# Window attention on one core: where the group statistic stands on VectorE, and which engine adds the bias of V

## The reference

```
x = x + _L0_conv_ref(_gn(x), L0_conv_w_qkv, L0_conv_b_qkv)

def _gn(v, G=32, eps=1e-05):
    g = v.reshape(B_, G, C_ // G, H_, W_)
    m = jnp.mean(g, axis=(2, 3, 4), keepdims=True)
    s = jnp.var(g, axis=(2, 3, 4), keepdims=True)
    return ((g - m) / jnp.sqrt(s + eps)).reshape(v.shape)

# _L0_conv_ref: roll by -3, -3; then
    qkv = jnp.einsum('bchw,oc->bohw', xs, w_qkv) + b_qkv[None, :, None, None]
    # cut into windows of 49 tokens and 8 heads
    scores = jnp.einsum('bxyhqd,bxyhkd->bxyhqk', q, k) * scale
    attn = jax.nn.softmax(scores, axis=-1)
    out = jnp.einsum('bxyhqk,bxyhkd->bxyhqd', attn, v)
    # back to b, c, h, w; roll by 3, 3
```

## Time and profile before

| | |
|---|---|
| median of 3 runs | 941.21 us (940.23 to 943.64) |
| the profiled execution | 941.08 us |
| its span, first to last instruction | 938.9 us |
| granted TensorE clock, mean | 0.99 |
| TensorE busy | 865.0 us, 92% |
| VectorE busy | 766.3 us, 82% |
| GpSimd busy | 739.3 us, 79% |
| ScalarE busy | 665.1 us, 71% |

### The profile page before, as it was taken

One profiled execution on the slowest core, in us unless ns is written; L12 is line 12 of the kernel. 1 busy time (PEld: TensorE's weight loads), 2 busy tenths in 40 slices (PEclk: granted clock), 3 DMA queues, 4 the chain that ended last, 5 costly groups with the idle time before them and its releaser, 6 DMA issues. The chain is left out here.

```text
span 938.9 us, 104445 instructions
## 1 busy us (share of the span) xinstructions
PE 865.0 (92%) x46473; PEld 708.7 (75%) x46473; DVE 766.3 (82%) x1399; ACT 665.1 (71%) x1297; POOL 739.3 (79%) x1191
## 2 busy tenths in 40 slices
PE   0479999998999999999999999999899999999994
PEld 0358888887788888887788888887678888888883
DVE  8657888889889888888888888888987777777873
ACT  2347777776677777777677777777677777777772
POOL 1347888887788888888788888888788888888883
PEclk9999999999999999999999999999999999999998
DMA  9401122112112211221211000000000000000001
GB/s 380 177 5 58 46 68 68 60 42 69 48 55 68 69 43 60 68 68 34 69 54 50 35 34 34 17 34 34 17 34 35 19 32 34 34 22 29 34 34 36
DMA packets 29912, 51.87 MB, mean 55 GB/s; under 512 B 3649, under 2 KB 28865, under 8 KB 29761
## 3 DMA queue, kind: packets, MB, share of 16 engines
q1 hardware_dynamic: 29888, 51.59, 15.8%
HBM read 25.89 MB, written 25.69 MB: 55 GB/s over the span
## 5 line engine op out<-in xcount | busy, mean ns | idle before, releaser
L373 ACT ACTIVATE probs_t<-psum,exp_scale 128x800 f32<-128x800 f32 x256 | 223.2, 923 | 139.6 <-PE psum L772 139.6
L571 DVE TENSOR_REDUCE neg_max<-psum 100x16 f32<-100x784 f32 x256 | 249.2, 974 | 39.1 <-PE psum L740 31.1
L291 POOL TENSOR_SCALAR mixed<-mixed,bias 128x392 f32<-128x392 f32 x128 | 161.7, 1263 | 123.2 <-DVE mixed L597 123.2
L740 PEld LDWEIGHTS psum<-k_hi,q_masks 32*128 32x128 f16 x8192 | 175.3, 91 | 46.3 <-issue 42.8
L740 PE MATMUL psum<-k_hi,q_masks 32*128 32x49 f16 x8192 | 197.8, 179 | 3.0 <-DVE neg_max L571 2.3
L740 PE MATMUL psum<-k_lo,q_masks 32*128 32x49 f16 x4096 | 182.6, 179 | 0.0
L740 PEld LDWEIGHTS psum<-k_lo,q_masks 32*128 32x128 f16 x4096 | 161.0, 91 | 0.0
L300 POOL TENSOR_TENSOR stage<-mixed,image 128x343 f32 (+7 forms) x256 | 144.2, 583 | 0.4 <-POOL mixed L291 0.4
L765 PE MATMUL psum<-q_masks,k_hi 32*64 32x100 f16 x8192 | 128.7, 219 | 16.1 <-DVE summed L588 13.3
L349 ACT ACTIVATE xn<-image,shift_c,rstd_c 128x21 f32 (+6 forms) x256 | 132.4, 573 | 8.0 <-DVE shift_c L551 6.1
L797 PE MATMUL psum<-probs_t,v_rows 64*32 64x100 f32 x8192 | 131.4, 252 | 2.4 <-issue 2.4
(11 more groups left out here) (112 smaller groups left out, 1828.2 us busy)
## 6 DMA issues: line engine op xcount, KB each, us to landing
out_dram<-stage SPq DMA_DIRECT2D x64, 224.0 KB, 2.1
out_dram<-stage SPq DMA_DIRECT2D x64, 168.0 KB, 1.9
image<-in_x_dram SPq DMA_DIRECT2D x32, 224.0 KB, 2.6
image<-in_x_dram SPq DMA_DIRECT2D x1, 6104.0 KB, 28.2
image<-in_x_dram SPq DMA_DIRECT2D x34, 168.0 KB, 2.5
image<-in_x_dram SPq DMA_DIRECT2D x6, 896.0 KB, 9.2
image<-in_x_dram SPq DMA_DIRECT2D x1, 728.0 KB, 14.3
w_nat<-in_L_conv_w_qkv_dram SPq DMA_DIRECT2D x1, 192.0 KB, 2.4
```

Source lines behind the costliest of these rows:

```text
L291: nc.gpsimd.tensor_scalar(mixed[:, half, :, :], mixed[:, half, :, :], bias[:, 2:3], None, ALU.add).then_inc(bias_added, 1)
L373: nc.scalar.activation(probs_t[:, 2 * u:2 * u + 2, :, :].rearrange("p h a q -> p h (a q)"), psum[:, COL_BANKS[u], 0:PAIRS * ROWS2], ACT.Ex ...
L571: nc.vector.tensor_reduce(neg_max[:, par, 2 * j:2 * j + 2, :], psum[0:ROWS2, ROW_BANKS, 0:GT] .rearrange("p h (w k) -> p h w k", k=TOK), A ...
L740: last = nc.tensor.matmul(psum[:, ROW_BANKS.start + h - 2 * j, w * TOK:(w + 1) * TOK], q_masks[rows, par, low + w * ROWS2:low + w * ROWS2 ...
```

## The change

Three things change.

1. On VectorE the statistic, and the pieces of the image change, stand behind `scale_rows`, directly ahead of the second maximum. Before, the statistic and one kind of piece stood behind the mask of Q, and another kind between `low_inverse` and `join`.
2. The image change begins two steps earlier and has one piece in each step, where six steps had up to two each. Its arithmetic is the same. Of the chunks of images 2 and 3, four steps now take two, where it was two steps.
3. The bias of V is added by ScalarE, in step g for group g-3, between the turned maximum and the exponentials. GpSimd adds the image to group g-4 in place of g-3, so each engine's program has one step more at the end.

```
@@ gpsimd
-            def add_bias(g, half):
-                pool.wait_ge(mixed_done, g + 2)
-                pool.sem_inc(waited, 1)
-                nc.gpsimd.tensor_scalar(mixed[:, half, :, :], mixed[:, half, :, :], bias[:, 2:3], None, ALU.add).then_inc(bias_added, 1)
...
             def step(g, n, par):
-                if live(g - 3):
-                    add_bias(g - 3, 1 - par)
                 if live(g - 1):
                     split_max(g - 1, 1 - par)
                 if live(g):
                     split_k(g, par)
-                if live(g - 3):
-                    add_image(g - 3, n - 2 + par, 1 - par)
+                if live(g - 4):
+                    add_image(g - 4, n - 2, par)
@@ scalar
+            def add_bias(g, half):
+                act.wait_ge(mixed_done, g + 2)
+                nc.scalar.activation(mixed[:, half, :, :], mixed[:, half, :, :], ACT.Identity, bias=bias[:, 2:3]).then_inc(bias_added, 1)
...
                     evac_neg(g - 1)
+                if live(g - 3):
+                    add_bias(g - 3, 1 - par)
                 if live(g - 1):
                     exp(g - 1, 0)
                     exp(g - 1, 1)
@@ vector
+            def norm_steps(b):
+                return [lambda: gather_channels(b), turn_channels, group_mean, group_variance] + NEWTON * [refine_root] + [lambda: offer(b)]
...
                 if live(g):
                     mask_q(g, par)
-                if ahead:
-                    ahead()
-                for chunk in chunks:
-                    take_stats(image_at + chunk * STAT, chunk)
                 if live(g - 2):
                     invert(g - 2)
                     low_inverse(g - 2)
-                if between:
-                    between()
...
                 if live(g - 2):
                     scale_rows(g - 2, par)
+                if ahead:
+                    ahead()
+                for chunk in chunks:
+                    take_stats(image_at + chunk * STAT, chunk)
                 if live(g):
                     maximum(g, par, 1)
...
             def change_image(b):
-                g = (b * BANDS - 4) * 2
-                for ahead, between in ((None, lambda: gather_channels(b)),
-                                       (turn_channels, group_mean),
-                                       (group_variance, guess_root),
-                                       (lambda: refine_root(1), lambda: refine_root(1)),
-                                       (lambda: refine_root(NEWTON - 2), scatter_groups),
-                                       (None, lambda: offer(b))):
-                    step(g, g // 2, g & 1, ahead=ahead, between=between)
-                    g += 1
+                first = (b * BANDS - 5) * 2
+                for g, piece in enumerate(norm_steps(b), first):
+                    step(g, g // 2, g & 1, ahead=piece)
...
-                for n in range(3):
+                for n in range(4):
                     dve.wait_ge(loaded[b + 1], 32 * -(-(2 * n + 2) * STAT // BAND))
                     two_steps(first + n, 2 * n, at)
                 dve.wait_ge(loaded[b + 1], 32 * BANDS)
-                for g in (2 * first + 6, 2 * first + 7):
-                    chunk = 6 + 2 * (g & 1)
-                    step(g, g // 2, g & 1, (chunk, chunk + 1), at)
-                with dve.Fori(4, CHUNKS // 2 - 1) as n:
-                    two_steps(n + first, 2 * n + 2, at)
+                with dve.Fori(4, CHUNKS // 2 - 4) as n:
+                    two_steps(n + first, 2 * n, at)
+                for n in (CHUNKS // 2 - 4, CHUNKS // 2 - 3):
+                    for par in range(2):
+                        chunk = CHUNKS - 8 + 4 * (n - CHUNKS // 2 + 4) + 2 * par
+                        step(2 * (first + n) + par, first + n, par, (chunk, chunk + 1), at)
```

More of the change, by code:

```diff
@@ L311, in step @@
                     split_k(g, par)
-                if live(g - 3):
-                    add_image(g - 3, n - 2 + par, 1 - par)
+                if live(g - 4):
+                    add_image(g - 4, n - 2, par)
                 if live(g + 2):
                     split_x(g + 2, par)
-            for g in range(-2, 4):
+            for g in range(-2, 6):
                 step(g, g // 2, g & 1)
-            with pool.Fori(2, GROUPS // 2 - 1) as n:
+            with pool.Fori(3, GROUPS // 2 - 1) as n:
                 step(2 * n, n, 0)
@@ L323, in _ @@
             pool.sem_inc(x_split, 1)
-            for g in range(GROUPS - 2, GROUPS + 3):
+            for g in range(GROUPS - 2, GROUPS + 4):
                 step(g, g // 2, g & 1)
@@ L423, in _ @@
                     step(2 * n + 1, n, 1, b)
-            for g in range(GROUPS - 2, GROUPS + 2):
+            for g in range(GROUPS - 2, GROUPS + 3):
                 step(g, g // 2, g & 1)
@@ L521, in group_mean, with refine_root, offer @@
                 link(nc.vector.tensor_tensor(work_b[:, :], work_a[:, :], work_a[:, :], ALU.mult))
+                link(nc.vector.tensor_tensor(work_a[:, :], work_b[:, :], var_row[:, :], ALU.add))
             def group_variance():
-                link(nc.vector.tensor_tensor(work_a[:, :], work_b[:, :], var_row[:, :], ALU.add))
                 link(nc.vector.tensor_reduce(g_var[:, :], grouped(work_a), AX.X, ALU.add))
                 link(nc.vector.tensor_scalar(g_var[:, :], g_var[:, :], 1.0 / PER, EPS, ALU.mult, ALU.add))
-            def guess_root():
                 link(nc.vector.tensor_scalar(half_bits[:, :], g_var[:, :].bitcast(i32), 1, None, ALU.logical_shift_right))
                 link(nc.vector.tensor_scalar(rs[:, :].bitcast(i32), half_bits[:, :], -1.0, float(0x5F3759DF), ALU.mult, ALU.add))
[L534 to L541, removed]
+            def refine_root():
+                link(nc.vector.tensor_tensor(rs_t[:, :], rs[:, :], rs[:, :], ALU.mult))
+                link(nc.vector.scalar_tensor_tensor(rs_t[:, :], rs_t[:, :], -0.5, g_var[:, :], ALU.mult, ALU.mult))
+                link(nc.vector.scalar_tensor_tensor(rs[:, :], rs_t[:, :], 1.5, rs[:, :], ALU.add, ALU.mult))
+            def offer(b):
+                wait(dve, xn_ready, (b - 1) * 2 * BANDS)
                 nc.vector.tensor_scalar(grouped(mean_row), g_sum[:, :, None].broadcast_to([C, 8, PER]), 1.0 / PER, None, ALU.mult)
                 link(nc.vector.tensor_scalar(grouped(var_row), rs[:, :, None].broadcast_to([C, 8, PER]), X_SCALE, None, ALU.mult))
-            def offer(b):
-                wait(dve, xn_ready, (b - 1) * 2 * BANDS)
                 nc.vector.transpose(mean_c[:, :], mean_row[:, :])
@@ L599, in scale_rows, with step @@
                                         summed[:, :, :].rearrange("p (s a) q -> p s a q", s=2), ALU.mult).then_inc(mixed_done, 1)
-            def step(g, n, par, chunks=(), image_at=None, ahead=None, between=None):
+            def step(g, n, par, chunks=(), image_at=None, ahead=None):
                 if live(g):
                     mask_q(g, par)
-                if ahead:
-                    ahead()
-                for chunk in chunks:
-                    take_stats(image_at + chunk * STAT, chunk)
                 if live(g - 2):
@@ L650, in _ @@
                     take_stats(chunk * STAT, chunk)
[L651 to L658, removed]
+            for piece in norm_steps(0):
+                piece()
             work_out_scales()
@@ L663, in _ @@
             step(1, 0, 1, range(5, 8), BANDS * BAND)
[L664 to L667, removed]
+            step(2, 1, 0, (8,), BANDS * BAND)
+            step(3, 1, 1, (9,), BANDS * BAND)
+            with dve.Fori(2, BANDS - 5) as n:
+                two_steps(n, 2 * n + 6, BANDS * BAND)
             for b in (1, 2):
```

## The result

The changed kernel takes 950.56 us, median of 4 runs (949.47 to 951.74), against 940.86 for the kernel before: a ratio of 1.0091, 95% interval 1.0064 to 1.0118. It is slower by 0.9%; forecast was 950.0. The profiled execution has a span of 948.9 us, 10.0 more than before.

The account below looks back on a forecast made before the run. TensorE's own order was taken to set a 6.69 us floor, exceeded by a 6.34 us loop plus pieces. 941.1 + 11.2 + 5.9 + 9.0 + 0.4 - 16.75 - 0.8 gave 950.0 us, range 935 to 959.

Parts of the forecast that it names:

- The loop: Row scores through second maximum and K's split to row scores: 6.34 us plus the inserted piece, against a 6.69 floor.
- The sum: Profiled execution 941.1 us plus 8.9: single statistics +11.2, doubles +5.9, image changes +9.0, start +0.4, removed waits -16.75, end -0.8.
- c: Time from the second maximum's end to the end of `k_lo` on GpSimd: 2.56 us, bounds 2.37 and 2.60.
- What goes: The 16.75 us lost in steady running disappear, as `join` no longer stands behind pieces.
- The bias on ScalarE: One more ScalarE operation, about 0.6 us, before the exponentials where it idles 0.95: no cost; later stores and loads not felt.
- The ends: First steps +0.4 us, bounds 0 and 2, mostly covered by code loads; end -0.8 from the shorter bias operation.
- What the profile would show: Periods 6.88, 7.4 and 6.9 to 7.3; some 25 us of TensorE waits naming `k_lo`; chain through L571, L282, L275.
- (A): Rival: GpSimd's split of the maximum gets in between the masks, 2.37 us to `k_lo`'s end; faster, 932.6 us; chance 0.15.
- (B): Rival: `inv_rows` on VectorE delays GpSimd's `k_lo` by 0.3 us in 17 steps; +5, 955 us; chance 0.11.

Follow-up runs that it names:

- e5: The changed kernel with each statistic taken over 224 columns in place of 448; 933.25 us, 0.9908 of the kernel before.
- e3: The changed kernel with GpSimd's split of K ahead of its split of the maximum; 927.62 us, 0.9819 of the kernel before.
- e1: The changed kernel with the bias of V back on GpSimd, one group earlier; 945.07 us, 1.0020 of the kernel before.
- e10: The kernel before with the bias on ScalarE, image added one group later, VectorE's full load wait and double statistics two steps later; 936.35 us, ratio 0.9936.
- e2: The kernel before with only the bias moved to ScalarE and the image added one group later; 944.67 us, ratio 1.0020.
- e4: The changed kernel with the statistics back behind the mask of Q; 934.10 us, 0.9889 of the kernel before.
- e13: The changed kernel plus one useless bias-sized GpSimd operation (1.26 us) in every step; 946.15 us, 1.0047 of the kernel before.

## Why the prediction was right

The forecast was 950.0, measured 950.56. By its own steps:

- **The loop, 6.34 us plus the piece.** Right in each term to 0.02. The rows above give 0.81 to the first maximum, 1.43 to `mixed`, 0.47 to the statistic; `k_lo` ends 2.57 after the maximum (forecast 2.56), the row scores follow 0.10 after it. e5 puts the threshold between 0.30 and 0.53, and the line through the points that cost at 0.35; e3 confirms that the way goes through GpSimd's order. A statistic counts 0.53 here, where 0.545 was taken from the start.
- **The sum.** Steps with one statistic 58 x 0.18 = 10.4 for 11.2; steps with two 8 x 0.71 = 5.6 for 5.9; three changes 9.3 for 9.0; 25.3 in all for 26.1, less 16.75. The single pieces came out nearly as priced: gathering takes 0.94 (period 7.29), turning 0.58, group mean and variance 0.89 and 0.83, the refinements 0.59 each (period 6.94 to 6.95) and the offer 0.71.
- **c, the disputed term.** Its value was right, and that it grows when the bias leaves. It was under-explored on the other side: with the bias on GpSimd and the statistic in its new place it is 2.26 (e1), less than my lower bound of 2.37.
- **What goes.** Right: `summed` is down to 0.8 us of waits, once.
- **The bias on ScalarE.** It takes 0.62 to 0.63 and costs ScalarE nothing: the idle time before the exponentials fell from 0.95 to 0.43, and e10 holds 6.69. That SP's and the loads' shift is not felt is right for this change only because the full wait moved along; e2 shows its price otherwise, two steps 3.8 and 4.2 us too long.
- **The ends.** The end is right, -0.8, and for the reason given: the image addition starts 0.83 after `mixed` ends, where it took 1.66. The sum behind step 127 by itself would not show it: e4 and e5 end in the same steps and have 24.9 and 23.3 us there. The start is mis-sized: +2.3 for +0.4, just over my bound of 2; that loads of code cover most of the moved statistics is shown by no run here. In step 1 TensorE waits 3.8 us for the low half of K in one piece; how much of the 2.3 that makes is open (see below). The errors of the start and of the sum (1.9 and -0.8) partly cancel; that the time came out closer than its terms is luck.
- **What the profile would show.** Periods as written. The names were wrong: I expected 25 us of waits put down to `k_lo`, and the view shows 3.8, once. The chain that ended last was to pass through L571, L282 and L275; the page of the profile puts 90% of it on TensorE and 0% on GpSimd. And `neg_halves` takes 0.56 in about half of the steps only. In the others it starts 0.34 instead of 0.18 after the maximum and takes 0.41; it ends 0.75 after the maximum in both.
- **Rivals.** (A) is refuted by c = 2.57 in the changed kernel; its mechanism is real and appears in e1 and e13. (B) does not happen as priced. In a step with two statistics `inv_rows` is asked for while GpSimd works on K's high part, ahead of `k_lo`:

```profile
402.19 0.28 DVE L576 SCALAR_TENSOR_TENSOR inv_rows<-inv_hi,low_rows,inv 128x49 f16<-128x49 f16 x1 [0.30 <-ACT inv_hi L381]
```

```profile
401.88 0.53 POOL L273 TENSOR_SCALAR k_hi<-k 128x392 f16<-128x392 f32 x1
402.50 0.90 POOL L275 TENSOR_TENSOR k_lo<-k,k_hi 128x392 f16<-128x392 f32 x1
```

It takes 0.28 and begins 0.31 into `k_hi`; neither delays the other, and it has just ended when `k_lo` starts. A trace of (B) is in two of the three changes, in one step each, where `inv_rows` is asked for just ahead of `k_lo`:

```profile
229.65 0.27 DVE L576 SCALAR_TENSOR_TENSOR inv_rows<-inv_hi,low_rows,inv 128x49 f16<-128x49 f16 x1 [0.38 <-ACT inv_hi L381]
...
229.72 0.96 POOL L275 TENSOR_TENSOR k_lo<-k,k_hi 128x392 f16<-128x392 f32 x1
```

There `k_lo` takes 0.96 for 0.91: 0.05 each time, where I had priced 0.3 in 17 steps. The Trainium skill, page SBUF — State Buffer, section Who interferes with whom, has a VectorE operation with two SBUF inputs contend with a GpSimd operation that reads SBUF. For `k_lo` the trace agrees: `inv_rows` asked for while it runs takes 0.56 to 0.81 us in the steps with one statistic (0.73 in the rows above) and ends 0.06 after it. For `k_hi`, which reads SBUF too, it doesn't.

**What made it slower, in one sentence.** No part does it alone in the single-statistic steps: the bias moved alone leaves 6.69 (e2, e10), so do the statistic and the pieces moved alone (e1), and together they give 6.87, because each takes a part of the same slack in the loop. With c = 2.26, as in e1, the loop without a piece is 6.03, 0.66 under 6.69; the statistic takes 0.53 of that and the move of the bias 0.31. The image change became cheaper (3.1 from 5.2), the doubles dearer and more.

**Open.** What the start owes to the moved statistics. Kernels whose first steps agree in VectorE's order differ by 4.4 us at step 5. The granted clock doesn't settle it. From 45 to 78 us its mean is 0.74 in the changed kernel and 0.90 before, but at 42 us it is the other way round, as the same matrix product shows, first before, then changed (0.53 is also what it takes in the changed kernel at 52 us, at 1.2 GHz):

```profile
42.37 0.53 PE L709 MATMUL psum<-xn_lo,w_hi 128*128 128x392 f16 x1
```

```profile
42.39 0.33 PE L698 MATMUL psum<-xn_lo,w_hi 128*128 128x392 f16 x1
```

Open too is why GpSimd's small operation is let in beside the masks only when an earlier GpSimd operation reaches far enough into them, and why the masks are held back at a reach of 0.39 and not at 0.15; the runs show that it is so, not how the access that the two engines share is granted.

## What to carry to other kernels

When an engine waits 0.2 us at some place, the work that can be put there free is not bounded by that wait but by the slack of everything behind it, around the loop: add up one whole round from start times in rows before moving work, and compare it with the period. Where the consumer (here the split of K) doesn't need what stands ahead of it on an in-order engine (the split of the maximum), swap the two first; that was worth 2.7% of the changed kernel's time here (ratios of 0.9819 and 1.0091 to the kernel before), more than any placing of the statistic. Look for a removed operation's side effects: taking 1.26 us a step off a 79% busy engine gained nothing in the steady steps and 0.6% in all without the moved statistic (e10, with the load's wait moved), and beside the moved statistic it cost 0.18 us in each of 58 steps.

## What the runs showed of the hardware

- Useless work made a kernel faster: 1.26 us more on GpSimd per step, 946.15 for 950.56 us, steady steps 6.69 for 6.87.
- A GpSimd operation of 32 elements asked for 0.3 us after VectorE's masks (800 elements, 16 bits) have begun takes 0.56 and ends 0.07 after them. It takes 0.23, during the masks, where another GpSimd operation reached 0.15 into them (e1, e13), and 0.32 where it reached 0.39; in the latter case the masks take 0.94 in place of 0.76. A reach of 0.03 to 0.09 changes nothing: 0.57.
- VectorE's `inv_rows`, with two inputs in SBUF, runs unhindered beside GpSimd's `k_hi` (one input, 0.28), but ends only with `k_lo` (two inputs) when it is asked for meanwhile: up to 0.81 in steps with one statistic.
- GpSimd's `k_hi`, asked for 0.25 us after the masks have begun, takes 0.89 in place of 0.53 (e3).
- TensorE's clock in the changed kernel: it is granted 2.4 GHz from 38.6 us, in the middle of row scores that began at 37.98. TensorE then stands idle from 42.90 to 46.72, and at 45.5, within that wait, it falls to 1.2 GHz, where it stays until 55.7. The two stretches in the view by stage (us; busy us and instructions of TensorE, its weight loads, VectorE, ScalarE, GpSimd; share of the full clock; DMA):

```profile
38.60:45.50 6.90, 3.12 (x94) 2.13 (x87) 5.70 (x10) 2.84 (x7) 1.87 (x4) 1.00 0.01 2
45.50:55.70 10.20, 7.89 (x296) 6.67 (x301) 4.64 (x8) 3.20 (x5) 5.04 (x9) 0.50 0.02 4
```
